# A layer-norm, scan and mixture-of-experts kernel: the first sequence's x is normalised by VectorE in place of ACT

## The reference

```python
xn = layernorm(x)                                  # (x - mean) / sqrt(var + 1e-5), over the 256 features
g, v, d = xn @ Wg + bg, xn @ Wv + bv, xn @ Wd + bd
a = 0.001 + 0.998 * sigmoid(d)
attn = linear_scan(sigmoid(g) * tanh(v), a)        # h[t] = a[t] * h[t-1] + x_scan[t], along the sequence
scores = sigmoid(xn @ Wr.T + br + bias)            # 8 experts, the two best are kept per token
ffn = sum over the two experts of score * (gelu(xn @ W1.T + b1) @ W2.T + b2)
shared = gelu(xn @ Ws1.T + bs1) @ Ws2.T + bs2
out = x + attn + shared + ffn
```

## Time and profile before

| | us |
|---|---|
| median of 3 runs | 690.43 (690.24 to 690.60) |
| the profiled execution | 689.23 |
| its span, first to last instruction | 687.4 |
| PE busy | 660.7 (96%) |
| DVE busy | 512.9 (75%) |
| ACT busy | 433.6 (63%) |
| POOL busy | 288.0 (42%) |

### The profile page before, as it was taken

The page is one execution under the profiler, slowest core; times in us unless marked ns, Lnnn a source line. Parts: engine busy times, 40 slices in busy tenths (PEclk is TensorE's granted clock), DMA queues, the critical chain, the costliest instruction groups (busy, mean ns, idle before and its releaser), DMA issues.

```text
span 687.4 us, 20158 instructions
## 1 busy us (share of the span) xinstructions
PE 660.7 (96%) x5872; PEld 521.4 (76%) x5873; DVE 512.9 (75%) x1334; ACT 433.6 (63%) x738; POOL 288.0 (42%) x261
## 2 busy tenths in 40 slices
PE   5899999999999998899999999999999999999995
PEld 4465757566666756788889888888889888898774
DVE  5899899999899889776666666666666666666653
ACT  6988696969696865455555555555555555554652
POOL 3133332414242634244546455454645445463512
PEclk9999999999999999999999999999999999999998
DMA  7534335252524231233334243333424333342412
GB/s 255 185 76 141 99 118 138 82 180 61 182 60 154 62 123 33 63 55 62 57 60 67 54 69 52 63 57 59 66 54 69 51 64 56 60 69 48 78 33 32
DMA packets 54173, 57.56 MB, mean 84 GB/s; under 512 B 13204, under 2 KB 48916, under 8 KB 54136
## 3 DMA queue, kind: packets, MB, share of 16 engines
q1 hardware_dynamic: 38456, 38.42, 18.8%
q0 software_dynamic: 15680, 18.69, 17.1%
HBM read 38.53 MB, written 18.55 MB: 83 GB/s over the span
## 4 chain that ended last, share of the span: by engine, by line
PE 84%; DVE 6%; issue 4%; DMA 2%; ACT 2%; POOLq 0%; SPq 0%; POOL 0%; DVEq 0%; ACTq 0%
PE bank L1239 34%; PE bank L1231 33%; PE bank L1219 7%; PE bank L1258 3%; PE bank L1288 2%; PE bank L1270 2%; DVE arena L897 1%; PE bank L1175 1%; DVE W L801 1%; PE bank L1210 1%; DMA arena<-in_gates 1%; DVE arena L898 1%; PE bank L1192 1%; PE bank L1184 1%; DVE arena L840 1%
## 5 line engine op out<-in xcount | busy, mean ns | idle before, releaser
L1239 PE MATMUL bank<-W,arena 128*128 (+1 forms) x2304 | 303.0, 273 | 4.0 <-DVE arena L898 4.0
L1231 PE MATMUL bank<-rows,W 128*128 128x256 f16 (+1 forms) x1920 | 298.5, 294 | 2.3 <-ACT arena L593 1.2
L1239 PEld LDWEIGHTS bank<-W,arena 128*128 128x128 f16 x2304 | 222.4, 98 | 41.9 <-DVE arena L898 4.0
L1231 PEld LDWEIGHTS bank<-rows,W 128*128 (+1 forms) x1920 | 185.8, 98 | 56.2 <-issue 2.9
L593 ACT ACTIVATE arena<-bank,par 128x256 f32<-128x256 f32 x256 | 137.0, 561 | 77.4 <-PE bank L1231 57.7
L506 POOL DMA_INDIRECT out<-arena,slot_add x64 | 109.7, 1714 | 150.9 <-ACT arena L730 141.2
L897 DVE TENSOR_SCALAR arena<-arena,par 128x256 f16<-128x256 f32 x284 | 101.4, 357 | 62.0 <-ACT arena L593 41.4
L898 DVE SCALAR_TENSOR_TENSOR arena<-arena,par 128x256 f16<-128x256 f32 x284 | 139.0, 489 | 10.0
L442 POOL DMA_INDIRECT lists<-entry,place x64 | 71.7, 1121 | 122.8 <-ACT arena L579 67.0
L491 POOL DMA_INDIRECT rows<-xhl_rows,slot_list x64 | 69.4, 1085 | 40.4 <-DMA slot_list<-lists 23.1
L601 ACT ACTIVATE rows<-bank 128x1024 f16<-128x1024 f16 x32 | 32.8, 1024 | 57.1 <-PE bank L1288 57.1
(11 more groups left out here) (162 smaller groups left out, 520.7 us busy)
## 6 DMA issues: line engine op xcount, KB each, us to landing
stage<-in_w SPq DMA_DIRECT2D x32, 512.0 KB, 4.8
b2row<-in_b SPq DMA_DIRECT2D x39, 128.0 KB, 2.9
arena<-in_x SPq DMA_DIRECT2D x8, 512.0 KB, 5.1
xhl_rows<-W SPq DMA_DIRECT2D x8, 512.0 KB, 4.6
out<-arena SPq DMA_DIRECT2D x8, 512.0 KB, 5.4
W<-in_w SPq DMA_DIRECT2D x4, 512.0 KB, 9.4
lists<-entry,place POOLq DMA_INDIRECT x64, 3.3
rows<-xhl_rows,slot_list POOLq DMA_INDIRECT x64, 2.8
```

The costliest lines, as they stand in the source:

```text
L1231: ins = T.matmul(bank_, weights(w, wp * HALF + c * H + j * P, P), rhs[:, 2 * xp + c, :], start=n == 0, stop=n == 3 * KD - 1)
L1239: ins = T.matmul(banks[t // 2][:, (t % 2) * D:(t % 2 + 1) * D], h[:, hp, t * P:(t + 1) * P], weights(w, (2 + wp) * HALF + j * D, D), start ...
```

## The change

The call of `normed(0, 0)` is gone from ACT's opening. A new function `normed_first` on DVE does the same for the first sequence, x times the reciprocal root plus the shift, tile by tile, with a wait for `rs_ok` before it; it is called between `variances(0, 0)` and `scales(None)`.

```diff
--- before.py
+++ after.py
@@ -699,7 +699,6 @@
                 c = slice(part * GCOL, (part + 1) * GCOL)
                 A(gw_flat[:, 0, c], graw[:, c], ACT.Square, accum_out=ssq[:, part:part + 1])
             A(ssq[:, 2:4], graw[:, 0:2], ACT.Square).then_inc(ssq_ok, 1)
-            normed(0, 0)
             x_high(0)
             act.wait_ge(scale_ok, 1)
             A(gw_flat[:, 0, :], graw, ACT.Copy, scale=scl[:, 0:1]).then_inc(whi_ok, 1)
@@ -816,6 +815,14 @@
                 own.mark(V.tensor_scalar(shift.unsqueeze(2), mv[:, :, 0:1], -1.0, None, ALU.mult))
                 V.tensor_scalar(ve.unsqueeze(2), mv[:, :, 1:2], EPS, XSCALE ** -2, ALU.add,
                                 ALU.mult).then_inc(var_ok, 1)
+
+            def normed_first():
+
+                dve.wait_ge(rs_ok, 1)
+                for t in range(TPB):
+                    ins = V.tensor_scalar(xs[:, t * D:(t + 1) * D], xt[0][:, t * D:(t + 1) * D], rs[:, t:t + 1],
+                                          shift[:, t:t + 1], ALU.mult, ALU.add)
+                ins.then_inc(xs_ok, 1)
 
             def x_low(b):
                 dve.wait_ge(xhi_ok, b + 1)
@@ -1088,6 +1095,7 @@
             own.mark(V.memset(PT[:, :, 3:4], 0.0))
             own.settle()
             variances(0, 0)
+            normed_first()
             scales(None)
             x_low(0)
             dve.wait_ge(whi_ok, 1)
```

## The result

The changed kernel takes 691.4 us (median of 16 runs, 690.67 to 692.33), the kernel before 689.9 beside it on the same chip (16 runs, 689.3 to 690.6). The ratio is 1.0022, with a 95% interval of 1.0015 to 1.0029 (written [1.0015, 1.0029] from here on): slower by 1.5 us. The interval excludes no change, which I had forecast; it includes the 0.2% that the prediction took as what a measurement can tell. The forecast of 690.4 stood on three runs of the kernel before, whose 16 runs beside the changed kernel have a median of 689.9.

The account below looks back on a forecast made before the run. PE was taken to bound the kernel, with 84% of the chain, its own queue ordering the opening. The terms summed to 0, 0 to -0.03 and 0, so 690.4 us, range 689.4 to 691.4.

Parts of the forecast that it names:

- (a): PE's opening transposes: the warm-up matmuls hold them until 11.76, so ACT's earlier finish gains 0.
- (b): First copy out of PSUM on ACT: needs the first eight transposes, still starts at 12.86; gain 0 to 0.03 us.
- (c): PE's logits: released by ACT's second copy, ended 14.80, so they still start at 14.91; gain 0.
- ACT's gap ahead of the copies: ACT in the opening: idle for 1.1 us before the first copy at 12.86, released by the transposes.
- The price on DVE: Four tensor-scalar operations added in DVE's opening: 1.0 us, between 0.75 and 1.40, hidden in idle time, cost 0.
- R2: Rival: DVE and POOL hold each other up in the opening; mild 690.5, chance 0.05; decisive 691.8 or more, 0.03.
- The room of 1.6 us: DVE's free time in the opening, from POOL's shift at 7.80 until the scales can start behind PE's sums at 9.39.
- scales after 9.6: Sign in DVE's opening: scales forecast at 9.43; a start after 9.6 would show DVE and POOL holding each other up.
- the mild R2: Rival: DVE's four operations let all POOL's small ones pass, x ready at 10.3; time 690.5, chance 0.05.
- Nothing else waits for what moved: Step beyond the opening's three terms: SP's store comes later anyway, POOL has 6 us of room; cost 0.
- R4: Rival: shifted ACT and DVE code moves an unreleased DVE gap onto or off the chain; 688.7 to 692.1, chance 0.06.
- the traces agree at 20 us and part later: Sign that shifted code, not the opening's work, changed the time, by up to 1.7 us either way.

Follow-up runs that it names:

- the short warm-up: First 24 warm-up matmuls half as wide: on the change with its count restored, 688.82 us in one execution; on the kernel before, 689.62, ratio 1.0002.
- the change with its count restored: The changed kernel with four opening DVE memsets merged into one and four one-column ACT copies added: 689.35 us, ratio 0.9993 [0.9984, 1.0002].

## Why the prediction was wrong

*The opening, (a), (b), (c): right in the order, and near enough in the sum.* The transposes start at 11.79, against 11.76 forecast, and the short warm-up confirms their holder by an experiment. The logits' releaser is ACT's copy in the profile after. ACT's gap ahead of the copies has come, but is 0.26 us and not 1.1. The 0 of (b) was not exact: I left PE's pace at 0.107 us a step, and where it rises during the transposes the first copy moves up, by 0.24 in the profile after and 0.47 in the change with its count restored. That kernel also confirms the sum: with all the work moved and no code shifted, ratio 0.9993 [0.9984, 1.0002], where the forecast was no change.

*The price on DVE: mis-sized, without effect.* I took 1.0 us for the four, within 0.75 to 1.40. They took 1.93, beyond the upper bound: 1.38 of their own, 0.55 from POOL beside them. The upper bound, from the batch statistics, was the right neighbour; what was missing was the allowance for contention, which R2 had beside the sum. The room of 1.6 us was overrun and the scales came 0.29 late. ACT's high half of x ended at 10.88, against 9.9 (at most 10.35) forecast, and the 1.1 us of spare time on ACT took it up. By the prediction's own sign (scales after 9.6) this is the mild R2, which gave 690.5 for far more; it cost nothing.

Of contention the Trainium skill says, in "SBUF — State Buffer", § "Who interferes with whom", that VectorE's second port pair is GpSimd's and is locked for one of them at a time. The 1.93 against 1.38, and the 0.38 against 0.17 of the conversion, are both of that direction; that a port is the cause was not isolated.

*"Nothing else waits for what moved": this step failed.* The shift of DVE's code by four instructions costs the whole 1.5 us. I let R4 stand for it with a chance of 0.06, and half of that within the bound. In the sum the term stood at nothing. The mechanism of R4 was named rightly, "if such a gap moved onto the chain", and so was its sign to look for, "the traces agree at 20 us and part later". What was wrong is how I weighed it. I argued that the gaps with no releaser sum to 3.8 us next to a chain that is 84% PE. But these rows list only gaps that show. A hole under a running scan of 1.23 us is no idle time and has no row: in the kernel before, the hole at record 319 is hidden so, and a sum over visible gaps can't tell how many hidden ones there are. What I needed was the sequencer's own records, which show a silence of 0.45 us behind the scan at 98 us and 0.09 behind the same scan one sequence later. With such holes 128 records apart in the program, and DVE's work in the sequences' stage directly ahead of PE's, each shift by a few instructions exposes some and covers others.

What the runs put in the place of the term: 0.25 at record 319, 0.30 at record 447, 0.13 at the same place of the loop's second trip near 192 us (L904 follows L816 by 0.24 there, by 0.11 before), and 0.4 to 0.5 from the two conversions moved against POOL's scatter: 1.1 to 1.2 of the 1.20 and 1.26 us that the two executions lose between 90 and 210. The rest of the 1.5 falls behind 265 us, the larger part near 630.

*Small slips in the working.* The chances that I named add up to 0.015 for faster and 0.045 for slower, and the 0.03 and 0.05 that I wrote add more on the fast side, against what the sentence says. The 0.71 us of L897 is the longest of 284 operations, not 142. Neither changes the forecast.

*What stays open.* Near 630 us PE waits for a gather of x, and this wait goes with the shift. In all four traces with four instructions more PE loses 0.4 to 0.6 us there for good. The waits of PE's weight loads for this gather are 0.4, 0.4, 0.6 and 0.6; with fourteen more it is 0.3, and in all the others there is none. In the changed kernel:

```profile
PEld bank L1296 <- DMA rows<-xhl_rows,small_list: 0.4, 1, 0.4
```

Together with the 1.2 before 265 us that is some 1.7, against 1.5 between the medians. What in the shifted code delays PE's gather I did not test. At the border of the stages (265 to 290 us) the kernels gain or lose up to 1.1 us, and two executions of the changed kernel differ by 0.35. Each step there is a transfer followed by the next. The chain of waits of the kernel before in its second execution, and of the changed kernel:

```profile
263.15 3.00 DMA lists<-entry,place
...
272.54 2.89 DMA rows<-xhl_rows,slot_list
```

```profile
264.12 3.56 DMA lists<-entry,place
...
273.58 3.77 DMA rows<-xhl_rows,slot_list
```

The same transfers take 0.6 and 0.9 us longer. Since the kernel before with the short warm-up also loses 0.4 there, with all of DVE's holes in their old places, I do not count the border as an effect of the change; nor is it shown that it is none.

Why the holes stand 128 records apart is open too. The Trainium skill says in "Runtime: NRT & Kernel Launch", § "Instruction fetch mechanics", that an engine fetches its instructions in blocks of 256 while it runs and that this is hidden by the pace at which it issues. The runs show places 128 records apart and silences of 0.34 us and more (some 0.1 on later trips of a loop), which are hidden only under a long operation. Whether they are these fetches, no run shows.

## What to carry to other kernels

Adding or removing instructions on an engine that feeds the bottleneck closely has a price of its own that has nothing to do with the work: here from nothing to 3.3 us for a shift of 2 to 14 instructions, and not in proportion to it. Before a small edit is judged by its time, run it once with the count on that engine restored (merge or add idle instructions ahead), and read the records of the sequencer for silences that a long operation covers. New operations are to be priced with what runs beside them: the four took 1.38 us alone and 1.93 next to POOL's.

## What the runs showed of the hardware that I had not expected

- DVE's sequencer is silent for 0.34 to 0.45 us in front of its record 319, whatever instruction stands there (16 of 17 traces), and again in front of 447 where no running operation hides it (0.44; with six instructions more it is missing). On a loop's later trips the hole is back at the same instruction with some 0.1 us, on every trip. Moving one onto the chain costs about 0.3; four instructions fewer on ACT cost nothing.
- A conversion of 128x8 takes 0.17 us when it starts 0.29 or 0.54 behind the start of POOL's indirect DMA (1.03 us long), and 0.35 to 0.38 when it starts 0.63 to 0.65 behind.
- POOL's first reduction over partitions starts at 16.39 and at 18.82 us in two executions of one kernel, and between 16.22 and 19.02 in all the traces where POOL's work before it ends by 10.2.
- PE's rise from steps of 0.107 us for 128 columns (1.2 GHz) to 0.056 (2.4 GHz) comes at another time in each execution: the 16 transposes took 1.24 and 1.67 us in two executions of the changed kernel, and 1.91 in both of the kernel before. It came during the transposes in six of the eight traces with the new operations and the full warm-up, and in none of the five without them. Whether that is chance, no run shows.
